# Moving the second batch's transposes and projections, and the modulation rows, into the score rounds of the head

## The reference, cut to what matters

```python
mod = (_silu(c) @ wmod).reshape(4, 6, 1, -1)
sa, ca, ga, sb, cb, gb = (mod[:, i] for i in range(6))
ga, gb = (sign(g) * maximum(abs(g), 0.25) for g in (ga, gb))
h = layernorm(x) * (1 + ca) + sa
x = x + ga * attention(h, Wqkv, bqkv, Wout, bout)      # 16 heads of 16, causal softmax
h = layernorm(x) * (1 + cb) + sb
x = x + gb * ffn(h)      # shared expert plus the top-1 routed expert
```

## Time and profile before

| what | value |
|---|---|
| three runs | 493.94 us median, 493.4 to 496.34 us |
| the profiled execution's own time | 495.28 us |
| its span | 493.5 us |
| granted TensorE clock, mean of the span | 0.94 |
| busy: PE, DVE, ACT, POOL | 83%, 64%, 46%, 43% of the span |
| instructions | 8599 |

### The profile page before, as it was taken

How to read it: one execution, slowest core, us unless ns; L and a number is a source line. 1 busy time by engine, 2 the same in 40 slices (tenths; PEclk the granted TensorE clock), 3 DMA queues, 4 the chain that set the end, 5 groups by cost and what they waited for, 6 DMA issues and landing times.

```text
span 493.5 us, 8599 instructions
## 1 busy us (share of the span) xinstructions
PE 409.6 (83%) x3009; PEld 231.0 (47%) x3009; DVE 313.9 (64%) x635; ACT 228.6 (46%) x407; POOL 211.8 (43%) x251
## 2 busy tenths in 40 slices
PE   4787965198977878998887987899998999999991
PEld 4233431044443534544443434457456666666661
DVE  7669372176749796899987783487973444443441
ACT  2623360287645766675566771635431233233220
POOL 2571395047403577235823275210060355546332
PEclk9979698589979999999899997999999999999998
DMA  8465364755757856675243200299371144343210
GB/s 270 150 156 118 110 153 96 244 193 187 179 138 239 265 189 147 154 223 173 85 164 119 55 2 0 90 374 343 121 223 48 33 91 75 81 87 68 44 21 0
DMA packets 46193, 67.97 MB, mean 138 GB/s; under 512 B 5380, under 2 KB 33668, under 8 KB 46152
## 3 DMA queue, kind: packets, MB, share of 16 engines
q1 hardware_dynamic: 40472, 58.76, 39.1%
q0 software_dynamic: 5152, 8.14, 8.2%
q10 hardware_dynamic: 528, 0.52, 0.3%
HBM read 43.14 MB, written 25.18 MB: 138 GB/s over the span
## 4 chain that ended last, share of the span: by engine, by line
PE 51%; DVE 18%; POOL 11%; issue 6%; ACT 6%; DMA 5%; SPq 2%; ACTq 0%; DVEq 0%; POOLq 0%
PE bank L1493 34%; DVE mx L1127 5%; PE bank L1653 3%; PE bank L1637 3%; DVE rowg L1228 2%; PE bank L1878 2%; PE bank L1585 2%; POOL W L762 2%; POOL W L743 2%; DMA w_d<-rowg 1%; DMA qk_d<-W 1%; PE bank L1608 1%; ACT rowg L940 1%; POOL rowg L770 1%; POOL rowg L769 1%
## 5 line engine op out<-in xcount | busy, mean ns | idle before, releaser
L890 ACT ACTIVATE W<-bank 128x512 f32<-128x512 f32 (+1 forms) x176 | 94.9, 565 | 70.5 <-PE bank L1637 69.1
L1127 DVE TENSOR_REDUCE mx<-bank 128x1 f32<-128x384 f32 (+3 forms) x176 | 105.2, 633 | 32.1 <-PE bank L1610 26.6
L1493 PE MATMUL bank<-W 128*128 128x256 f16 (+2 forms) x756 | 107.8, 296 | 4.9 <-DVE x_sb L1172 2.1
L1493 PEld LDWEIGHTS bank<-W 128*128 128x128 f16 x756 | 74.2, 101 | 38.7 <-issue 10.0
L762 POOL TENSOR_SCALAR_AFFINE_SELECT W<-W 128x512 f32<-128x512 f32 x64 | 46.2, 725 | 103.3 <-ACT W L890 103.1
L1637 PE MATMUL bank<-W 128*128 128x512 f16 (+3 forms) x256 | 65.8, 315 | 24.2 <-ACT W L890 18.6
L1493 PE MATMUL bank<-W,h2T 128*128 x276 | 67.3, 380 | 1.7 <-DVE W L1243 1.0
L833 POOL DMA_INDIRECT out<-h2T,sidx x23 | 36.3, 1578 | 63.9 <-DVE h2T L1463 63.6
L1653 PE MATMUL bank<-W 128*32 128x128 f32 (+3 forms) x512 | 49.7, 463 | 13.8 <-POOL W L762 13.8
L1608 PE MATMUL bank<-W 126*128 126x128 f16 (+3 forms) x208 | 54.8, 315 | 6.9 <-DVE mx L1127 6.8
L1637 PEld LDWEIGHTS bank<-W 128*128 128x128 f16 x256 | 22.2, 100 | 61.7 <-ACT W L890 34.7
(11 more groups left out here) (172 smaller groups left out, 554.3 us busy)
## 6 DMA issues: line engine op xcount, KB each, us to landing
w_d<-rowg SPq DMA_DIRECT2D x18, 512.0 KB, 3.0
W<-w_d SPq DMA_DIRECT2D x18, 512.0 KB, 7.9
stage<-in_gup SPq DMA_DIRECT2D x16, 512.0 KB
qk_d<-W SPq DMA_DIRECT2D x48, 128.0 KB
W<-qk_d SPq DMA_DIRECT2D x32, 192.0 KB, 4.4
stage<-in_down SPq DMA_DIRECT2D x8, 512.0 KB
x_sb<-in_x SPq DMA_DIRECT2D x4, 512.0 KB, 9.5
h_d<-gbb SPq DMA_DIRECT2D x4, 512.0 KB, 5.3
```

The costliest lines, as they stand in the source:

```text
L890: a.activation(PT[j][:, i:i + m, :], t_bank(N)[:, 0:m * w].rearrange("p (i n) -> p i n", i=m), ACT.Exp).then_inc(s_exp, 1)
L1127: v.tensor_reduce(mx_v[:, b % 2, hp0 // 4, par, i:i + m, t], s_bank(N)[:, 0:m * w].rearrange("p (i n) -> p i n", i=m), AX.X, ALU.max).then ...
L1493: i = t_.matmul(outp, l, r, start=(n == 0), stop=(n == len(prods) - 1), **kw)
```

## The change

Eight things change, most of them places in the tables:

1. The first batch's `v` goes from steps 17 and 24 of the head to 13 and 17, with one PSUM bank for each part; VectorE moves them out at 17 and 21.
2. The second batch's `turn` goes from step 33 to step 24.
3. The second modulation matmul goes from step 20 to step 28, ScalarE's copy from 22 to 28, and GpSimd's arithmetic from steps 1 and 3 of round 0 to steps 30 and 31 of the head.
4. The second batch's four `qk` parts go to steps 33, 36, 40 and 42 of the head (before: 39, 40 and, in round 0, 1 and 3), and `NEXT` goes away.
5. `low_others` goes from step 36 of the head to step 8 of round 0.
6. The pieces' splits are numbered anew: round 0 has six (4, 9, 14, 18, 22, 26) where it had seven (2, 6, 10, 15, 19, 23, 28), round 3 seven where it had six.
7. SyncE does `qk_out(1, 0)` before the first load, and puts the other two loads and the modulation rows between the second batch's writes and stacks.
8. The waits for PSUM banks follow from `take_bank` alone.

```diff
 SPLITS = {-1: {},
-          0: {2: 0, 6: 1, 10: 2, 15: 3, 19: 4, 23: 5, 28: 6},
-          1: {2: 7, 6: 8, 10: 9, 15: 10, 19: 11, 23: 12},
-          2: {2: 13, 7: 14, 14: 15, 19: 16, 22: 17, 28: 18, 33: 19, 38: 20},
-          3: {5: 21, 8: 22, 14: 23, 18: 24, 23: 25, 28: 26}}
-FIRST = [(0, 3, 7), (7, 10, 13), (13, 15, 18)]
+          0: {4: 0, 9: 1, 14: 2, 18: 3, 22: 4, 26: 5},
+          1: {2: 6, 6: 7, 10: 8, 15: 9, 19: 10, 23: 11},
+          2: {2: 12, 7: 13, 12: 14, 16: 15, 20: 16, 23: 17, 28: 18, 33: 19},
+          3: {1: 20, 5: 21, 8: 22, 14: 23, 18: 24, 23: 25, 28: 26}}
+FIRST = [(0, 2, 6), (6, 9, 12), (12, 14, 18)]
-HEAD = [(17, "v", 0, 0), (24, "v", 0, 1), (32, "max", 0, 0), (33, "turn", 1, 0), (33, "turn", 1, 1),
-        (39, "qk", 1, 0), (40, "qk", 1, 1)]
-NEXT = [(1, "qk", 1, 2), (3, "qk", 1, 3)]
+HEAD = [(13, "v", 0, 0), (17, "v", 0, 1), (24, "turn", 1, 0), (24, "turn", 1, 1), (28, "mod", 0, 1),
+        (32, "max", 0, 0), (33, "qk", 1, 0), (36, "qk", 1, 1), (40, "qk", 1, 2), (42, "qk", 1, 3)]
...
             if c == 1 and job == "qk":
-                return [M1, M0][k % 2]
+                return [M0, M1][k % 2]
+            if (c == 0 and job == "v") or (c == 1 and job == "turn"):
+                return [M1, M0][k]
+            if job == "mod":
+                return [T0, M0][k]
...
             maxima(0, 0)
-            for k in range(3):
-                stage_load(k)
             qk_out(1, 0)
+            stage_load(0)
+            sp.wait_ge(s_m4, 1)
+            sp.dma_start(mod_d[:, :], m4[:, :]).then_inc(s_md, 16)
             stacks(1, 0)
             qk_out(1, 1)
-            stacks(1, 1)
-            sp.wait_ge(s_m4, 1)
-            sp.dma_start(mod_d[:, :], m4[:, :]).then_inc(s_md, 16)
+            stage_load(1)
             sp.wait_ge(s_md, 16)
             mod_rows(0)
+            stacks(1, 1)
+            stage_load(2)
             sp.dma_start(gbb[:, :, :], mod_d[:, 3 * H:4 * H].partition_broadcast(P)).then_inc(s_gbb, 16)
...
-                    if b == 0 and n in (1, 3):
-                        modulation_rows(n == 3)
+                    if b < 0 and n in (30, 31):
+                        modulation_rows(n == 31)
...
-                    if b < 0 and n == 22:
+                    if b < 0 and n == 28:
                         modulation_rows(1)
                         other_high()
...
-                    if b < 0 and n in (21, 28):
-                        v_out(0, n == 28)
-                    if b < 0 and n == 36:
+                    if b < 0 and n in (17, 21):
+                        v_out(0, n == 21)
+                    if b == 0 and n == 8:
                         low_others()
...
-                if c == 1:
-                    pe.wait_ge(s_q32, 2)
...
-                if (job, c, k) == ("qk", 1, 1):
-                    pe.wait_ge(s_mr, 2)
-                elif used:
+                if used:
                     pe.wait_ge(*released(*used[-1]))
...
-                    if b < 0 and n == 20:
-                        modulation_rows(1)
```

More of the change, by code:

```diff
@@ L117, in side_jobs @@
     jobs = [(job, b + d, part) for at, job, d, part in SIDE if at == n and 0 <= b + d < B]
-    if b == 0:
-        jobs += [(job, c, part) for at, job, c, part in NEXT if at == n]
     if b == B - 1:
@@ L431, in side_bank @@
             if c == 1 and job == "qk":
-                return [M1, M0][k % 2]
+                return [M0, M1][k % 2]
[3 more added lines that the diff above has]
+                return [T0, M0][k]
             return tail[job][k] if c == B - 1 and job in tail else M1
         def released(job, c, k):
-            return {"down": (s_ye, TT * c + 2 * (k + 1)),
+            return {"down": (s_ye, TT * c + 2 * (k + 1)), "mod": (s_mr, k + 1),
                     "max": (s_neg, 2 * c + k + 1), "v": (s_v, TT * c + 2 * (k + 1)),
@@ L961, in modulation_rows @@
                     ac.wait_ge(s_wl, 1)
-                a.activation(mraw[:, 512 * c:512 * (c + 1)], [T0, M0][c][0:B, :], ACT.Copy).then_inc(s_mr, 1)
+                a.activation(mraw[:, 512 * c:512 * (c + 1)], side_bank("mod", 0, c)[0:B, :], ACT.Copy).then_inc(s_mr, 1)
             h_parts(0, 0)
@@ L1092, in v_out @@
                     dst = v1[b % 2][:, NH * 17 * t:NH * 17 * (t + 1)].rearrange("p (h d) -> p h d", d=17)
-                    src = M1[:, H * (t % 2):H * (t % 2 + 1)].rearrange("p (h d) -> p h d", d=HD)
+                    src = side_bank("v", b, k)[:, H * (t % 2):H * (t % 2 + 1)].rearrange("p (h d) -> p h d", d=HD)
                     v.scalar_tensor_tensor(dst[:, :, 0:HD], src, 1.0 / WS,
@@ L1506, in modulation_rows @@
                 pe.wait_ge(s_wmr[c], 16)
-                if c == 1:
-                    pe.wait_ge(s_q32, 2)
                 for k in range(KC):
-                    i = t_.matmul([T0, M0][c][0:B, :], cs[:, 1, k], wm[:, k, 512 * (c + 1):512 * (c + 2)],
+                    i = t_.matmul(side_bank("mod", 0, c)[0:B, :], cs[:, 1, k], wm[:, k, 512 * (c + 1):512 * (c + 2)],
                                   start=(k == 0), stop=(k == KC - 1))
@@ L1542, in project_v @@
                     sl = slice(P * t, P * (t + 1))
-                    i = split_mm(M1[:, H * (t % 2):H * (t % 2 + 1)],
+                    i = split_mm(side_bank("v", b, half)[:, H * (t % 2):H * (t % 2 + 1)],
                                  [(h1[:, 0, k, sl], h1[:, 1, k, sl], wq16[:, 0, k, 2 * H:3 * H],
@@ L1748, in _ @@
                 project_qk(0, u)
-            last_job.append(("qk", 0, 0))
+            last_job.extend([("qk", 0, 0), ("qk", 0, 1)])
             for b in range(-1, B):
@@ L1779, in _ @@
                     for job, c, k in side_jobs(b, n):
-                        if job in ("max", "v", "attn", "turn", "out", "qk", "h2", "route", "down"):
+                        if job in ("mod", "max", "v", "attn", "turn", "out", "qk", "h2", "route", "down"):
                             take_bank(job, c, k)
@@ L1783, in _ @@
                             max_turn(c, k)
+                        elif job == "mod":
+                            modulation_rows(k)
                         elif job == "v":
```

## The result

The changed kernel took 479.09 us (median of four runs, 475.92 to 481.22), the kernel before 493.91 us: a ratio of 0.9685 with a 95% interval from 0.9619 to 0.9751, or 14.8 us less. The forecast was 481.0 us in a range from 472 to 488. Four more runs beside the experiments gave 478.13 us and a ratio of 0.970 (0.9644 to 0.9757). The profiled execution took 478.08 us; its span is 476.3 us, 17.2 us less than before.

What follows compares the result with a forecast made beforehand. Stretches with all engines still, mainly 20 us in round 0's first 14 steps behind GpSimd's arithmetic and SyncE's list; -11.5 - 0.6 - 2.0 + 1.2 = -12.9 us from 495.28 gives 482.4, less 1.3 for the median: 481.0 us, range 472 to 488.

Steps and rivals of the forecast that it cites:

- GpSimd's arithmetic: Modulation arithmetic moved into the head: starts at 47.0, takes 12.9 us, ends at 59.9.
- SyncE's list: Second batch's writes, stacks and loads followed in order: write of piece 0 issued at 78.0, ten us earlier than 88.37.
- The head up to the modulation matmul: TensorE's head up to step 28: modulation matmul starts at 44.5, including 2.3 us for VectorE's late maxima; 42.3 if hidden.
- 12.0 us that I had estimated by the page: GpSimd's arithmetic in the head beside maxima out of PSUM: some 0.9 us of 12.9 would go, sum -13.8 us.
- signs of being wrong: Exponential 0 far later than 65, waits for loads of pieces 0 and 1, or a longer second half of round 0.
- The landing: Write of piece 0 lands between 85.2 and 90, taken as 87.6; exponential 15 starts at 89.2, -11.5 us.
- The rest of round 0: After step 14: three splits instead of four, -0.6 us, and an earlier end of the round, -2.0 us.
- The one split less: Round 0 after step 14 has three splits where it had four: half of 1.2 us, -0.6 us (bounds 0 and -1.2).
- The end of the round: End of round 0: last halves_out at step 26, not 28, shortens the 3.7 us stall: -2.0 us.
- GpSimd's part: End of round 0: the third batch's second qk part, at step 25, is not ready much earlier, limiting the gain.
- Rounds 1 to 3: Rounds 1 and 2 unchanged; one more split in round 3 costs +1.2 us (bounds 0 and 1.2).
- the larger gain: Rival, chance 0.15: piece 0's write lands at 81, exponential 15 at 84.2 (-16.5), sum -21.4, 472.5 us.

Runs made afterwards that it cites:

- second trace of the changed kernel: The changed kernel itself, nothing altered, timed again beside further variants of SyncE's list: 478.13 us, ratio 0.970.
- first version: Changed kernel with loads of pieces 1 and 2 and piece 0's write ahead of modulation rows, second stacks and gates' rows in SyncE's list: 475.96 us, ratio 0.9655.
- both edits together: Changed kernel with the SyncE list edits of the first version and the second version: 471.65 us, ratio 0.955.
- third version: Both edits together, plus second stacks moved behind the third piece's write and gates' rows behind the fourth's: 472.97 us, ratio 0.9499.
- the last: The third version with the second batch's third and fourth qk parts back at steps 1 and 3 of round 0: 471.57 us, ratio 0.9476.
- second version: Changed kernel with the third batch's first stacks behind the second batch's maxima in SyncE's list of round 0: 473.15 us, ratio 0.959.
- third session: The timing session in which the kernel before took 496.59 us; it included the third version and the last.

## Why the prediction was right, and where its terms were off

The mechanism held step by step: GpSimd's arithmetic off round 0, SyncE's list earlier, the same wait at a later step. The median came out 1.9 us below the forecast; but the sum was made for the profiled execution, and there it is 17.2 us beside the forecast 12.9, so 4.3 us off. The prediction had added the 1.3 us between profiled execution and median of before; after the change the median lay 1.0 us above the profiled execution. The closer of the two hits is luck. By its own terms:

- **The head up to the modulation matmul.** Forecast 44.5, measured 40.7. The 2.3 us charged for VectorE's late maxima were not paid, and even the 42.3 for that case was 1.6 us too late. I had taken twelve matmuls of the first `v` at the lower clock, twice 1.48 us; in the changed kernel they took 1.48 us. Between 28 and 35 us the granted clock was 1.00, before it was 0.51 (over the first 60 us 0.98 and 0.86).
- **GpSimd's arithmetic.** Forecast 12.9 us, measured 11.5 us (43.28 to 54.77), no operation longer than 1.08 us. In the Trainium skill the page "SBUF — State Buffer", section "SBUF: two separate sides", says that VectorE instructions with two SBUF inputs and GpSimd instructions that read SBUF block each other. Beside maxima out of PSUM nothing was stretched; the trace agrees, and the 12.0 us that I had estimated by the page were nearer than the sum of the old rows. I had missed a second stretched operation before the change: at 72.08 line 723 took 1.34 us beside `split_low(1)`, 0.72 us elsewhere. With its 0.6 us too the estimate is 11.4 us. The four `qk_low` and the table load then took as forecast: exponential 0 came 5.1 us after the arithmetic by the forecast, 5.0 us by the trace. So the forecast start "near 65" was 5.2 us late, for the two reasons above.
- **SyncE's list.** Forecast 78.0 for the write of piece 0, measured 75.02. The two terms before it had brought 5.1 us, and the list gave back 2.1: from the end of the arithmetic it took 18.1 us by the forecast (59.9 to 78.0) and 20.2 us by the trace (54.8 to 75.0), because six writes took 4.77 us of the queue instead of 3.65 and the second landing 5.23 instead of 3. The waits of 1.61 and 3.11 us for the loads of pieces 0 and 1 were one of the prediction's own signs of being wrong: the queue was fuller than I thought. They did no harm, because the wait at step 14 came last in any case; in the run with the old list they are absent and exponential 15 is later.
- **The landing.** Forecast 9.6 us, the middle between 7.2 and 12; measured 8.63. Exponential 15: forecast -11.5 us, measured -16.0, of which 3 us come from the earlier issue of the write and 1.5 from less time in the landing and behind it.
- **The rest of round 0.** Forecast -2.6 us, measured +0.6 (0.0 in the second trace of the changed kernel). This is the step that failed, in both of its terms. The one split less, priced at -0.6, brought nothing: from exponential 15 to the end of 43 it took 34.8 us, before 33.8, and with the old tables and seven splits also 33.8. Where the 1.0 us is lost is not shown. The end of the round, priced at -2.0, moved by 0.5. The third batch's writes did start earlier, 13.7 instead of 12.1 us before the end of exponential 43. But the three landings that follow one another behind them took longer: 5.00, 4.95 and 1.78 us (lines above), before

```profile
125.95 4.48 DMA qk_d<-W
...
132.28 4.57 DMA ng_d<-negm
...
137.14 1.53 DMA W<-ng_d
```

Together that is 1.15 of the 1.6 us; in the second trace of the changed kernel it is 0.8. I had priced the start and taken the landings as fixed. Why they took longer is not shown. GpSimd's part, which I had named as a limit, now does stand in the chain ahead of the last two writes,

```profile
107.44 1.17 POOL W L745
108.61 0.78 SPq L509
```

but the six writes took 4.31 us with it, before 4.41, so it did not take the gain.
- **Rounds 1 to 3.** Forecast 0 and +1.2 us, measured -0.4 and, clock apart, 0.0. The split added to round 3 at its step 1 is hidden.

The larger gain of the first half (4.5 us) and the missing gain of the rest of round 0 (3.2 us) have opposite signs and partly cancelled; the sum was better than its terms. The rest of the 4.3 us is the 1.2 that round 3 did not cost, its 1.4 of clock and 0.4 in round 2. Of the rivals, the larger gain was nearest for the first half (-16.0 against -16.5), for another reason than it gave: the write did not land in 3 us, it was issued earlier.

## What to carry to other kernels

Where all engines stand still, follow the in-order list of the queue that issues the transfers: here one write of a piece stood behind a chain of landings that did not concern it. Put small transfers that an engine waits for ahead of bulk that is needed a dozen steps later, on both counts: the place in the list, and the bytes queued ahead of it. And price a moved job by what comes after it up to the next wait, not by its own end: nine microseconds won before exponential 0 were worth nothing, until the landing behind them was gone. And where a stall is long enough to bring the granted clock down, its price is more than its idle time: here about 1.8 us more in the stretch behind it.

## What had not been expected

What was queued ahead of a transfer counted for more than its size here. For step 22 the maxima's write of 16 KB took 9.6 and 10.1 us behind four stack reads and four transfers of 512 KB (first version, and both edits together), 2.4 us in the third version and 4.1 us in the last. At the end of round 0 it took 5.0 us behind four stack reads and 1.4 us without them (changed kernel and second version). Writes of a piece, 512 KB, took 2.9 us where little was ahead, and 8.6 us behind the stacks.

And the start of the routed experts' loop showed in all four kernels of the third session a longer stop before the same matmuls: TensorE idle 3.9 to 4.0 us instead of 1.03, for a result of VectorE, whose own idle time of 2.8 us the profile gives to "issue". The clock fell with it: the 48 matmuls behind took 6.3 to 7.1 us instead of 5.40. From exponential 175 to the end these traces are 4.6 to 5.3 us longer than the others' 178 us, whatever their edit. The kernel before was 3 us slower in that session; no trace of it was taken there, so that it is the same stop is not shown. It is a reason not to compare microseconds between sessions.
